# A recommendation tower: GpSimd's pair products and diagonals wait for VectorE's adds, with four diagonal buffers and z0 in one VectorE instruction

## The chip, the cores and the metric

The kernel runs on one core of a Trainium2 chip. The metric is the device time of one execution, in microseconds (us). The core has TensorE (PE, with its weight loads PEld), VectorE (DVE), ScalarE (ACT), GpSimd (POOL) and the queue engine SyncE (SP), each with a program of its own; they meet through semaphores.

## The reference

512 samples have 39 looked-up embeddings of 16 numbers each. Three layers of a compressed interaction network (CIN) follow, then two dense layers and an output.

```python
e = jnp.stack([tbl_f[ids[:, f]] for f in range(39)], axis=1)      # B=512, F=39, D=16

def cin_layer(X0, Xi, W, b):                                      # H = 128
    Wr = W.reshape(H, F0, Fi)
    return jnp.einsum('hjk,bjd,bkd->bhd', Wr, X0, Xi) + b[None, :, None]

Xi, res = e, []
for W, b in Ws:                       # three layers
    Xi = cin_layer(e, Xi, W, b)
    res.append(Xi.sum(axis=2))        # z0, z1, z2: 128 wide each
h = jnp.concatenate([*res, dense_ctx], axis=1)
h = relu(h @ W_top1 + b_top1); h = relu(h @ W_top2 + b_top2); y = h @ W_top3
```

Everything is float32.

## The kernel before

A column is one pair (sample, d); 512 × 16 columns make 16 groups of 512 columns (32 samples), and a group is four tiles of 128 columns (s = 0 to 3, eight samples each). All engines run the same loop over groups g, tiles s and ten chunks c of a tile; p = 10 s + c is the chunk's number in its group. The first group, the last and the two or three before it are written out, the others are one hardware loop. While group g is worked on, the first CIN layer of group g+1 is prepared, and the embeddings of group g+2 are gathered.

*TensorE.* `t_chunk` (L433) makes 512 columns of the second layer's weights times x1 (384 in chunk 9) in one of five PSUM banks, with three matmuls (high and low parts, L444 to L446). It waits until the chunk that used the bank five chunks before has been scaled. In between come: seven `pair_product`s for the next group (L412), after the chunks of `PAIR_AT`; four transposes of the next x0 after chunk 8 (L420); and after chunk `G_AT` of a tile the small product `g_product` (L429), x2 of two tiles before times a diagonal.

*ScalarE* scales chunks 0, 1, 3, 5, 7, 9 by x0t (L579), one instruction for each of the up to four 128-wide units of a chunk; it also copies x0t (L544), the small products (L566), and makes x1 of the next group with its bias and high part (L552, L561).

*VectorE* does chunks 2, 4, 6, 8 as multiply-adds onto ScalarE's results (L672, four instructions a chunk). Between them stand the five adds that sum the tile before over j (`sum_over_j`, L693): 1536 elements ("big"), 768, 384, 128 and a last 128 into x2, placed by `SUM_AT`; and the low part of x1 (L661, `lo`).

*GpSimd*, in this order within a group: `form_pairs` (L345) multiplies two factors of 117 × 512 for the next group's seven pair products, at the chunks of `FORM_AT` (6, 10, ..., 30); `diagonal` (L332) spreads x0t of a tile over a mask, at chunk 5 of each tile; `gather` (L322) issues ten indirect DMAs, at `GATHER_AT`; `index` makes their addresses at chunk 37; and `sum_z0` (L354, L357) sums x1 over d for z0 by halving, after tile 1. A position p in the code only orders GpSimd's own instructions. What they wait for are data and free buffers: a pair product for its factors and for the buffer of the pair two before it, a diagonal for the small product of two tiles before.

*SP* waits until all seven pairs of a group are formed and its gathers have landed, stores the gathered rows to scratch memory, loads them again as `rep`, copies `rep` twice and three times to `first`, and then six times to `second`; the first pair product of the next group waits for that chain.

After the last group the third layer's sum over all j follows in one block, then the dense layers.

Of the kernel before, what the change touches and what calls it, by code (L numbers as in the profile page):

```python
# [24 lines left out]
B, F, D, H = 512, 39, 16, 128  # L25
P = 128
# [30 lines left out]
RED = 5  # L57
# [13 lines left out]
FORM_AT = [6 + 4 * b for b in range(BLOCKS)]  # L71
PAIR_AT = [p + 5 for p in FORM_AT]
X0T_AT = 8
AHEAD = 2
GATHER_AT = [1, 3, 7, 9, 13, 15, 19, 21, 25, 27]
INDEX_AT = 37
G_AT = 5
G_COPY_AT = 7
# [3 lines left out]
HALVINGS = 3  # L82
Z0_TILE = 1
SUM_AT = (1, 3, 5, 6, 7)


def tower_program(nc, ids, starts, table, dense_t, pair_a, pair_b, w1, w2, b0, b1, b2,
# [6 lines left out]
    with ctx:  # L94
# [19 lines left out]
        diag = sb("diag", [P, 2, TB, J1])  # L114
# [50 lines left out]
        g_psum = small_bank[:, 0:TB * J1].rearrange("p (b j) -> p b j", b=TB)  # L165
# [24 lines left out]
        halved = sem("halved")  # L190
# [116 lines left out]
        def _(pool):  # L307
# [18 lines left out]

            def diagonal(t, slot, first):

                pool.wait_ge(x0t_ready, t + 1)
                if not first:  # L330
                    pool.wait_ge(g_mm, t - 1)
                pool.tensor_tensor(  # L332
                    diag[:, slot % 2, :, :],
                    x0t[:, slot:slot + 1, :].to_broadcast([P, TB, J1]),
                    mask[:, :].unsqueeze(2).to_broadcast([P, TB, J1]), ALU.mult).then_inc(diag_ready, 1)
# [11 lines left out]

            def sum_z0(g):

                pool.wait_ge(x1_lo_ready, (g + 1) * len(PIECES))  # L350
                by_d = x1[:, :].rearrange("p (b d) -> p b d", d=D)
                n, halvings = D // 2, 0
                while n > 1:
                    pool.tensor_tensor(by_d[:, :, 0:n], by_d[:, :, 0:n], by_d[:, :, n:2 * n], ALU.add).then_inc(halved, 1)  # L354
                    n, halvings = n // 2, halvings + 1
                    pool.wait_ge(halved, g * HALVINGS + halvings)
                pool.tensor_tensor(z0[:, bass.ds(g * GB, GB)].unsqueeze(2), by_d[:, :, 0:1], by_d[:, :, 1:2],  # L357
                                   ALU.add).then_inc(z0_ready, 1)
# [9 lines left out]
            def group(g, first=False, last=False, gathers=True, then_index=True):  # L368
                for s in range(TILES_PER_GROUP):
                    t = g * TILES_PER_GROUP + s  # L370
                    for c in range(CHUNKS):
                        p = s * CHUNKS + c
                        if c == G_AT:
                            diagonal(t, s, first and s < 2)
                        if p in FORM_AT and not last:
                            form_pairs(g + 1, FORM_AT.index(p))
                        if p in GATHER_AT and gathers:
                            gather(GATHER_AT.index(p))
# [414 lines left out]
```

## Time and profile before

| | us |
|---|---|
| median of 3 timed runs | 769.84 (767.8 to 770.15) |
| the profiled execution: its time | 767.13 |
| its span (first to last instruction) | 765.3 |
| TensorE busy | 674.8 (88%) |
| VectorE busy | 644.9 (84%) |
| ScalarE busy | 505.4 (66%) |
| GpSimd busy | 503.5 (66%) |

The span is the time between the first and the last instruction in the trace; some 2 us lie around it. Busy time doesn't count waits, but an instruction that has started and is held up counts as busy. The mean granted TensorE clock is 0.969 of full speed.

### The profile page before, as it was taken

What the parts mean: (1) busy time and instruction counts of PE and PEld (TensorE: products, weight loads), DVE (VectorE), ACT (ScalarE), POOL (GpSimd) and SP (SyncE); (2) the same over time, 40 slices, a digit from 0 to 9 for tenths busy, and PEclk for the clock granted to TensorE, in tenths of its full rate; (3) what the DMA queues carried; (4) which work ended last, traced back from release to release, by engine and by line L of the source; (5) the groups of instructions that cost most, each with busy time, mean ns of one, the idle gap of its engine ahead of it and who ended that gap; (6) DMA issues with size and microseconds to landing.
All of it is one profiled execution on the core that took longest, in us unless ns stands there. A gap on an engine that the chain in (4) does not pass through costs nothing. (4 is left out here: it accounts for less than half of the span.)

```text
span 765.3 us, 12277 instructions
## 1 busy us (share of the span) xinstructions
PE 674.8 (88%) x2525; PEld 470.0 (61%) x2525; DVE 644.9 (84%) x1425; ACT 505.4 (66%) x1700; POOL 503.5 (66%) x437
## 2 busy tenths in 40 slices
PE   2678999889898989989898979799898989999898
PEld 0246766657575757657675756576665667775463
DVE  0448899879898997999898989789899889999890
ACT  2055777658584966767585858577676758797572
POOL 6739596676859594967677685958688674422830
PEclk9899999999999998999999999999999999999999
DMA  6452121212121212212131312112130212000310
GB/s 194 95 147 54 32 80 15 82 23 74 28 69 40 69 40 43 67 20 84 16 86 20 77 29 69 40 39 70 20 90 10 78 28 78 23 1 1 92 39 0
DMA packets 54165, 41.34 MB, mean 54 GB/s; under 512 B 33735, under 2 KB 39092, under 8 KB 54023
## 3 DMA queue, kind: packets, MB, share of 16 engines
q1 hardware_dynamic: 49030, 39.72, 18.0%
q0 software_dynamic: 5120, 1.47, 3.4%
q8 instruction: 5, 0.08, 0.0%
q14 instruction: 10, 0.07, 0.0%
HBM read 10.46 MB, written 1.28 MB: 15 GB/s over the span
## 5 line engine op out<-in xcount | busy, mean ns | idle before, releaser
L579 ACT ACTIVATE prod<-t_bank,x0t 128x128 f32<-128x128 f32 x1472 | 415.7, 387 | 173.2 <-PE t_bank L446 168.6
L672 DVE SCALAR_TENSOR_TENSOR prod<-t_bank,x0t,prod 128x128 f32<-128x128 f32 x1024 | 286.0, 339 | 47.3 <-PE t_bank L446 46.8
L444 PE MATMUL t_bank<-w_hi,x_hi 128*128 128x512 f32 (+1 forms) x640 | 312.0, 487 | 15.4 <-DVE prod L672 12.2
L322 POOL DMA_INDIRECT emb<-in_table,idx x160 | 218.4, 1365 | 61.8 <-issue 54.9
L445 PE MATMUL t_bank<-w_lo,x_hi 128*128 128x512 f32 (+1 forms) x640 | 252.6, 395 | 0.0
L446 PE MATMUL t_bank<-w_hi,x_lo 128*128 128x512 f32 (+1 forms) x640 | 251.9, 394 | 0.0
L444 PEld LDWEIGHTS t_bank<-w_hi,x_hi 128*128 128x128 f32 x640 | 124.2, 194 | 79.7 <-DVE prod L672 22.4
L412 PE MATMUL x_bank<-pairs,w_pair 117*128 117x512 f32 x224 | 123.8, 636 | 46.4 <-POOL pairs L345 44.2
L693 DVE TENSOR_TENSOR partial<-partial 128x768 f32<-128x768 f32 (+2 forms) x192 | 155.7, 811 | 0.1
L445 PEld LDWEIGHTS t_bank<-w_lo,x_hi 128*128 128x128 f32 x640 | 124.3, 194 | 48.2 <-issue 27.6
L693 DVE TENSOR_TENSOR partial<-prod 128x1536 f32<-128x1536 f32 x64 | 132.7, 2073 | 15.2 <-ACT prod L579 9.0
L332 POOL TENSOR_TENSOR diag<-x0t,mask 128x320 f32<-128x320 f32 x64 | 58.4, 912 | 124.4 <-PE small_bank L429 124.4
L446 PEld LDWEIGHTS t_bank<-w_hi,x_lo 128*128 128x128 f32 x640 | 123.6, 193 | 25.0
L345 POOL TENSOR_TENSOR pairs<-first,second 117x512 f32<-117x512 f32 x90 | 121.6, 1351 | 4.8 <-PE x_bank L412 1.7
L412 PEld LDWEIGHTS x_bank<-pairs,w_pair 117*128 117x128 f32 x224 | 40.5, 194 | 70.5 <-POOL pairs L345 55.8
L566 ACT ACTIVATE G<-small_bank 128x320 f32 (+1 forms) x64 | 48.2, 753 | 6.4 <-PE small_bank L429 6.4
L693 DVE TENSOR_TENSOR x<-partial 128x128 f32<-128x128 f32 x64 | 47.7, 746 | 3.4
L354 POOL TENSOR_TENSOR x<-x 128x256 f32<-128x256 f32 (+2 forms) x48 | 48.0, 1000 | 3.0
L429 PE MATMUL small_bank<-diag,x 128*128 128x320 f32 x128 | 45.0, 432 | 1.6 <-DVE x L693 1.6
L727 DVE TENSOR_TENSOR w_hi<-G,w_hi 128x512 fp32r<-128x512 f32 x39 | 32.9, 912 | 2.3 <-ACT w_hi L627 2.3
L345 POOL TENSOR_TENSOR pairs<-first,rep 117x512 f32<-117x512 f32 x15 | 23.2, 1549 | 16.7 <-DMA first<-rep 16.7
L627 ACT ACTIVATE w_hi<-G 128x512 fp32r<-128x512 f32 x39 | 24.2, 631 | 8.7 <-PE t_bank L513 7.2
(66 smaller groups left out, 271.7 us busy)
## 6 DMA issues: line engine op xcount, KB each, us to landing
second<-rep SPq DMA_DIRECT2D x96, 234.0 KB
first<-rep SPq DMA_DIRECT2D x48, 78.0 KB
emb<-in_table,idx POOLq DMA_INDIRECT x160
G<-in_w SPq DMA_DIRECT2D x1, 2496.0 KB
w_ring<-in_w SPq DMA_DIRECT2D x13, 192.0 KB, 2.4
rep<-rep SPq DMA_DIRECT2D x28, 78.0 KB
rep<-emb_scratch SPq DMA_DIRECT2D x20, 78.0 KB
emb_scratch<-emb SPq DMA_DIRECT2D x16, 78.1 KB
```

Of the source, the lines that this page charges most:

```text
L322: pool.indirect_dma_start(out=emb[:, i * D:(i + 1) * D], out_offset=None, in_=table, in_offset=bass.IndirectOffsetOnAxis(ap=idx[:, i:i + 1 ...
L332: pool.tensor_tensor(diag[:, slot % 2, :, :], x0t[:, slot:slot + 1, :].to_broadcast([P, TB, J1]), mask[:, :].unsqueeze(2).to_broadcast([P, ...
L345: pool.tensor_tensor(pairs[:, b % 2, :], first[:, :], rep[0:PAIRS, :] if b == 0 else second[:, k, :], ALU.mult).then_inc(pair_ready, 1)
L354: pool.tensor_tensor(by_d[:, :, 0:n], by_d[:, :, 0:n], by_d[:, :, n:2 * n], ALU.add).then_inc(halved, 1)
L412: pe.matmul(x1_bank[:, :], w_pair[:, b * H:(b + 1) * H], pairs[:, b % 2, :], start=b == 0, stop=b == BLOCKS - 1).then_inc(pair_mm, 1)
L444: pe.matmul(acc, hi, w1_hi[:, cols], start=True, stop=False)
L445: pe.matmul(acc, hi, w1_lo[:, cols], start=False, stop=False)
L446: pe.matmul(acc, lo, w1_hi[:, cols], start=False, stop=True).then_inc(t_mm, 1)
L566: act.activation(G[:, :, bass.ds(g * GB + s * TB, TB)].rearrange("p j b -> p b j"), g_psum, ACT.Copy).then_inc(g_copied, 1)
L579: last = act.activation(prod[:, s % 2, SLOT[c] + u, :], t_bank[c % T_BANKS][:, u * H:(u + 1) * H], ACT.Copy, scale=x0t[:, s, j:j + 1])
L672: last = dve.scalar_tensor_tensor(unit, t_bank[c % T_BANKS][:, u * H:(u + 1) * H], x0t[:, s, j:j + 1], unit, ALU.mult, ALU.add)
L693: dve.tensor_tensor(out, left, right, ALU.add).then_inc(summed, 1)
```

## The change

- GpSimd's `form_pairs` and `diagonal` first call the new `beside_multiplies(t, c)`: they wait until VectorE has done the adds that stand before chunk c in its program. The positions `FORM_AT`, `PAIR_AT`, `DIAG_AT`, `GATHER_AT`, `SUM_AT` and `G_AT` move.
- `diag` has four buffers in place of two, and its axes are exchanged (j outer, sample inner), as are those of the small product in PSUM; ScalarE's copy of it no longer permutes. The diagonal waits for the small product of four tiles before.
- z0 moves from four adds on GpSimd (with semaphores between) to one `tensor_reduce` on VectorE, at chunk 4 of the group.

```diff
--- before.py
+++ after.py
@@ -68,20 +68,20 @@
 TOP1, TOP2 = 512, 256
 M1, M2 = TOP1 // P, TOP2 // P
 
-FORM_AT = [6 + 4 * b for b in range(BLOCKS)]
-PAIR_AT = [p + 5 for p in FORM_AT]
+FORM_AT = [6, 8, 12, 18, 22, 28, 32]
+PAIR_AT = [9, 11, 15, 21, 25, 31, 35]
+DIAG_AT = [2, 14, 24, 34]
 X0T_AT = 8
 AHEAD = 2
-GATHER_AT = [1, 3, 7, 9, 13, 15, 19, 21, 25, 27]
+GATHER_AT = [2, 2, 2, 8, 8, 14, 18, 20, 24, 28]
 INDEX_AT = 37
-G_AT = 5
-G_COPY_AT = 7
+G_AT = 2
+G_COPY_AT = 5
 BIAS_AT = 5
 X1_LO_AT = 36
 X1_LO_LAST_AT = 2
-HALVINGS = 3
-Z0_TILE = 1
-SUM_AT = (1, 3, 5, 6, 7)
+Z0_AT = 4
+SUM_AT = (2, 4, 6, 6, 8)
 
 
 def tower_program(nc, ids, starts, table, dense_t, pair_a, pair_b, w1, w2, b0, b1, b2,
@@ -111,7 +111,7 @@
         first = sb("first", [PAIRS, COLS])
         second = sb("second", [PAIRS, SECOND_SLOTS, COLS])
         x0t = sb("x0t", [P, TILES_PER_GROUP, J1])
-        diag = sb("diag", [P, 2, TB, J1])
+        diag = sb("diag", [P, TILES_PER_GROUP, J1, TB])
         pairs = sb("pairs", [PAIRS, 2, COLS])
         x1 = sb("x1", [P, COLS])
         x1_hi = sb("x1_hi", [P, COLS], f32r)
@@ -162,7 +162,7 @@
         small_bank = pb("small_bank", [P, COLS])
         h1_bank = [x1_bank, x0t_bank, t_bank[2], t_bank[3]]
         h2_bank = [t_bank[1], t_bank[4]]
-        g_psum = small_bank[:, 0:TB * J1].rearrange("p (b j) -> p b j", b=TB)
+        g_psum = small_bank[:, 0:TB * J1].rearrange("p (j b) -> p j b", b=TB)
         x0t_psum = x0t_bank[:, 0:TILES_PER_GROUP * F].rearrange("p (s f) -> p s f", f=F)
 
 
@@ -187,7 +187,6 @@
         x1_ready = sem("x1_ready")
         x1_hi_ready = sem("x1_hi_ready")
         x1_lo_ready = sem("x1_lo_ready")
-        halved = sem("halved")
         z0_ready = sem("z0_ready")
         t_mm = sem("t_mm")
         act_scaled = sem("act_scaled")
@@ -324,15 +323,22 @@
                     in_offset=bass.IndirectOffsetOnAxis(ap=idx[:, i:i + 1], axis=0),
                 ).then_inc(gathered, 16)
 
+            def beside_multiplies(t, c):
+
+                done = sum(at < c for at in SUM_AT)
+                if isinstance(t, int) and (t - 1) * RED + done <= 0:
+                    return
+                pool.wait_ge(summed, (t - 1) * RED + done)
+
             def diagonal(t, slot, first):
 
                 pool.wait_ge(x0t_ready, t + 1)
                 if not first:
-                    pool.wait_ge(g_mm, t - 1)
+                    pool.wait_ge(g_mm, t - TILES_PER_GROUP + 1)
                 pool.tensor_tensor(
-                    diag[:, slot % 2, :, :],
-                    x0t[:, slot:slot + 1, :].to_broadcast([P, TB, J1]),
-                    mask[:, :].unsqueeze(2).to_broadcast([P, TB, J1]), ALU.mult).then_inc(diag_ready, 1)
+                    diag[:, slot, :, :],
+                    x0t[:, slot, :].unsqueeze(2).to_broadcast([P, J1, TB]),
+                    mask[:, :].unsqueeze(1).to_broadcast([P, J1, TB]), ALU.mult).then_inc(diag_ready, 1)
 
             def form_pairs(g, b):
 
@@ -345,18 +351,6 @@
                 pool.tensor_tensor(pairs[:, b % 2, :], first[:, :], rep[0:PAIRS, :] if b == 0 else second[:, k, :],
                                   ALU.mult).then_inc(pair_ready, 1)
 
-            def sum_z0(g):
-
-                pool.wait_ge(x1_lo_ready, (g + 1) * len(PIECES))
-                by_d = x1[:, :].rearrange("p (b d) -> p b d", d=D)
-                n, halvings = D // 2, 0
-                while n > 1:
-                    pool.tensor_tensor(by_d[:, :, 0:n], by_d[:, :, 0:n], by_d[:, :, n:2 * n], ALU.add).then_inc(halved, 1)
-                    n, halvings = n // 2, halvings + 1
-                    pool.wait_ge(halved, g * HALVINGS + halvings)
-                pool.tensor_tensor(z0[:, bass.ds(g * GB, GB)].unsqueeze(2), by_d[:, :, 0:1], by_d[:, :, 1:2],
-                                   ALU.add).then_inc(z0_ready, 1)
-
             for g in range(AHEAD):
                 index(g, first=g == 0)
                 for i in range(GATHERS):
@@ -370,16 +364,18 @@
                     t = g * TILES_PER_GROUP + s
                     for c in range(CHUNKS):
                         p = s * CHUNKS + c
-                        if c == G_AT:
-                            diagonal(t, s, first and s < 2)
+                        if p in DIAG_AT:
+                            beside_multiplies(t, c)
+                            diagonal(t, s, first)
                         if p in FORM_AT and not last:
+                            beside_multiplies(t, c)
                             form_pairs(g + 1, FORM_AT.index(p))
-                        if p in GATHER_AT and gathers:
-                            gather(GATHER_AT.index(p))
+                        if gathers:
+                            for i, at in enumerate(GATHER_AT):
+                                if at == p:
+                                    gather(i)
                         if p == INDEX_AT and then_index:
                             index(g + AHEAD + 1)
-                    if s == Z0_TILE:
-                        sum_z0(g)
 
             group(0, first=True)
             with pool.Fori(1, GROUPS - AHEAD - 1) as g:
@@ -427,7 +423,7 @@
                 if not (isinstance(t, int) and t == 0):
                     pe.wait_ge(g_copied, t)
                 pe.matmul(small_bank[:, 0:TB * J1], x2[:, slot % 2, :],
-                          diag[:, slot % 2, :, :].rearrange("p b j -> p (b j)"),
+                          diag[:, slot, :, :].rearrange("p j b -> p (j b)"),
                           start=True, stop=True).then_inc(g_mm, 1)
 
             def t_chunk(t, s, c, first_tile, then_x0t):
@@ -453,7 +449,7 @@
                         p = s * CHUNKS + c
                         t_chunk(t, s, c, first and s == 0, g + 1 if p == X0T_AT and not last else None)
                         if c == G_AT and not (first and s < 2):
-                            g_product(t - 2, s)
+                            g_product(t - 2, (s - 2) % TILES_PER_GROUP)
                         if not last:
                             if p == X0T_AT:
                                 transpose_x0(g + 1, False)
@@ -480,7 +476,7 @@
             with pe.Fori(1, GROUPS - 1) as g:
                 group(g)
             group(GROUPS - 1, last=True)
-            g_product(TILES - 2, 0)
+            g_product(TILES - 2, 2)
 
 
 
@@ -495,7 +491,7 @@
                     pe.wait_ge(act_scaled, TILES * NA)
                     pe.wait_ge(dve_scaled, TILES * ND)
                 if m == M1 - 1:
-                    g_product(TILES - 1, 1)
+                    g_product(TILES - 1, 3)
                 first_layer(m, P, 0, z0[:, :], start=True)
                 first_layer(m, D, 3, dense[:, :])
 
@@ -563,8 +559,7 @@
             def copy_g(t, g, s):
 
                 act.wait_ge(g_mm, t + 1)
-                act.activation(G[:, :, bass.ds(g * GB + s * TB, TB)].rearrange("p j b -> p b j"),
-                               g_psum, ACT.Copy).then_inc(g_copied, 1)
+                act.activation(G[:, :, bass.ds(g * GB + s * TB, TB)], g_psum, ACT.Copy).then_inc(g_copied, 1)
 
             def scale_chunk(t, s, c, first):
 
@@ -673,6 +668,12 @@
                                                     x0t[:, s, j:j + 1], unit, ALU.mult, ALU.add)
                 last.then_inc(dve_scaled, 1)
 
+            def sum_z0(g):
+
+                dve.wait_ge(x1_ready, g + 1)
+                dve.tensor_reduce(z0[:, bass.ds(g * GB, GB)], x1[:, :].rearrange("p (b d) -> p b d", d=D),
+                                  AX.X, ALU.add).then_inc(z0_ready, 1)
+
             def sum_over_j(t, slot, i, first):
 
                 if i == 0:
@@ -703,8 +704,11 @@
                             split_x1_lo(g + 1, 0)
                         if p == X1_LO_LAST_AT:
                             split_x1_lo(g, 1)
-                        if c in SUM_AT and not (first and s == 0):
-                            sum_over_j(t - 1, s + 1, SUM_AT.index(c), first and s < 3)
+                        if p == Z0_AT:
+                            sum_z0(g)
+                        for i in range(RED):
+                            if SUM_AT[i] == c and not (first and s == 0):
+                                sum_over_j(t - 1, s + 1, i, first and s < 3)
 
             dve.wait_ge(w_loaded, 16 * 3)
             dve.tensor_tensor(w_pair[:, :], pair_a_raw, pair_b_raw, ALU.add).then_inc(w_pair_ready, 1)
```

## Rows read from the trace of the kernel before

**Rows 1.** Busy time by stretch: groups 1 to 13, then group 14.

```profile
93.30:638.34 545.04, 492.27 (x1899) 354.64 (x1899) 493.17 (x1120) 381.34 (x1340) 394.61 (x335) 0.97 0.21 50
638.34:674.62 36.28, 36.11 (x148) 26.72 (x147) 35.21 (x88) 29.24 (x105) 16.20 (x15) 1.00 0.14 46
```

**Rows 2.** Costliest groups of instructions, on the page: the GpSimd work of the change.

```profile
L332 POOL TENSOR_TENSOR diag<-x0t,mask 128x320 f32<-128x320 f32 x64 | 58.4, 912 | 124.4 <-PE small_bank L429 124.4
...
L345 POOL TENSOR_TENSOR pairs<-first,second 117x512 f32<-117x512 f32 x90 | 121.6, 1351 | 4.8 <-PE x_bank L412 1.7
...
L354 POOL TENSOR_TENSOR x<-x 128x256 f32<-128x256 f32 (+2 forms) x48 | 48.0, 1000 | 3.0
```

**Rows 3.** Waits over the span: us in total, times, longest.

```profile
DVE prod L672 <- PE t_bank L446: 46.8, 26, 5.3
PE x_bank L412 <- POOL pairs L345: 44.2, 21, 3.5
```

**Rows 4.** The line of VectorE's adds: ns at least, median, at most.

```profile
L693 DVE TENSOR_TENSOR partial<-prod x64: 1757/1759/3677, 54.6 to 704.7; 128x1536 f32<-128x1536 f32 x64
```

**Rows 5.** VectorE's timeline: start, duration, instruction, idle before it.

```profile
259.08 1.76 DVE L693 TENSOR_TENSOR partial<-prod 128x1536 f32<-128x1536 f32 x1
...
260.76 1.12 DVE L672 SCALAR_TENSOR_TENSOR prod<-t_bank,x0t,prod 128x128 f32<-128x128 f32 x4
...
262.00 0.95 DVE L693 TENSOR_TENSOR partial<-partial 128x768 f32<-128x768 f32 x1
...
263.90 0.55 DVE L693 TENSOR_TENSOR partial<-partial 128x384 f32<-128x384 f32 x1
...
267.31 1.80 DVE L693 TENSOR_TENSOR partial<-prod 128x1536 f32<-128x1536 f32 x1
...
275.23 2.22 DVE L693 TENSOR_TENSOR x<-partial 128x128 f32<-128x128 f32 x1
...
609.68 1.13 DVE L672 SCALAR_TENSOR_TENSOR prod<-t_bank,x0t,prod 128x128 f32<-128x128 f32 x4 [1.59 <-PE t_bank L446]
...
646.06 1.76 DVE L693 TENSOR_TENSOR partial<-prod 128x1536 f32<-128x1536 f32 x1
```

**Rows 6.** GpSimd's timeline.

```profile
249.53 1.27 POOL L345 TENSOR_TENSOR pairs<-first,second 117x512 f32<-117x512 f32 x1
...
263.87 1.72 POOL L345 TENSOR_TENSOR pairs<-first,rep 117x512 f32<-117x512 f32 x1 [0.34 <-DMA first<-rep]
...
267.32 1.21 POOL L322 DMA_INDIRECT emb<-in_table,idx  x1 [0.30 <-issue]
...
274.73 1.24 POOL L322 DMA_INDIRECT emb<-in_table,idx  x1 [0.19 <-issue]
...
276.00 1.29 POOL L345 TENSOR_TENSOR pairs<-first,second 117x512 f32<-117x512 f32 x1
...
646.08 2.89 POOL L345 TENSOR_TENSOR pairs<-first,second 117x512 f32<-117x512 f32 x1 [1.74 <-PE x_bank L412]
```

**Rows 7.** TensorE's timeline.

```profile
286.27 2.08 PE L412 MATMUL x_bank<-pairs,w_pair 117*128 117x512 f32 x2 [2.58 <-POOL pairs L345]
...
607.73 1.12 PE L412 MATMUL x_bank<-pairs,w_pair 117*128 117x512 f32 x2 [1.15 <-POOL pairs L345]
...
638.44 0.39 PE L446 MATMUL t_bank<-w_hi,x_lo 128*128 128x512 f32 x1
...
639.12 0.39 PE L446 MATMUL t_bank<-w_hi,x_lo 128*128 128x512 f32 x1
...
640.12 0.40 PE L445 MATMUL t_bank<-w_lo,x_hi 128*128 128x512 f32 x1
...
644.91 1.02 PE L412 MATMUL x_bank<-pairs,w_pair 117*128 117x512 f32 x2
```

**Rows 8.** Stretches with the granted clock (the share after the five engines).

```profile
287.00:291.00 4.00, 4.00 (x10) 2.81 (x9) 1.23 (x5) 0.38 (x2) 3.49 (x3) 0.50 0.04 2
608.00:612.00 4.00, 4.00 (x17) 2.81 (x16) 2.38 (x9) 1.72 (x6) 3.79 (x4) 1.00 0.22 62
```

## The prediction

> **What bounds the kernel now.** I read the stretch windows first. From VectorE's first multiply-adds of group 1 to those of group 14 lie 545.0 us, 13 groups that also gather, 41.93 us each. Group 14, which forms pairs but gathers nothing, takes 36.28, and TensorE is busy for 36.11 of it [rows 1]. So 36.3 is TensorE's own work for a group, and 5.6 us a group are lost elsewhere. The reader should see two losses. Pair products and the z0 sums on GpSimd are dear [rows 2], and the list of waits shows TensorE idle for GpSimd's pairs (44.2 us) and VectorE idle for TensorE (46.8) [rows 3]. And VectorE's adds stretch: the 1536-element add lasts 1.76 us at least, 3.68 at most [rows 4]. The timelines show what stretches them: the 128-element add of 275.23 took 2.22 and ended right behind the pair product of 276.00 to 277.29; the big add of 646.06, begun 0.02 before a pair product, kept its 1.76, and the pair product took 2.89 [rows 5, 6]. A gather alone leaves an add alone (1.80 against a gather of 1.21 [rows 5, 6]). So VectorE is delayed by GpSimd, TensorE by both, and all three are near their limit in turn.
>
> **The steps, part by part.** Times below are counted in one steady group from TensorE's chunk 0; I follow the instructions in order, because mean busy time can't tell which wait ends last.
>
> Prices. A chunk is 0.68 us of TensorE; the small product adds about 0.55; from a pair product that TensorE waited for to the next chunk's multiply-adds are 1.95 (607.73 to 609.68), to the next chunk's slot about 1.67 [rows 5, 7]. On VectorE, start to start: big add 1.68, four multiply-adds 1.04, 768 add 0.87; the 384 and 128 adds in a row about 0.9 with their wait [rows 5]. GpSimd: pair 1.27 to 1.29, diagonal 0.9 on average, gather 1.24 plus 0.2 to 0.3 between [rows 2, 6]; the last pair of a group to the first of the next 13.07 (250.80 to 263.87), the DMA chain through the scratch [rows 6]. A hand-over to GpSimd by semaphore I take as 0.1, an estimate: TensorE's pair product of 644.91 ended at 645.93 and GpSimd's of 646.08 began 0.15 later [rows 6, 7].
>
> *z0.* GpSimd loses the four adds: 48.0 us for three of the four kinds over 16 groups, 3.0 each [rows 2], plus gaps. VectorE gains one reduction over 512 elements. The trace has none. Bounds: the 384-element add, 0.55, and the 1536-element add, 1.76 [rows 5]; it is nearest the first, by the slope between them 0.68. It delays the first pair of the next group by as much, since it stands before the 768 add. With 1.76, each group would be 1.1 longer.
> "VectorE: DVE Perf Modes", section Rules for kernel authors, of the Trainium skill advises against this step: a reduction has only the plain mode and is called the slowest operation. Here the fp32 adds run at the same 1.05 ns an element [rows 5], so by the rule as by the row the sum stays 0.68.
>
> *The waits.* Pair products at chunks 8, 18, 28 now wait until VectorE has done the 384 and 128 adds behind the multiply-adds of chunk 6 of the same tile; those at 2 wait for the last add of the tile before, the one at 6 for the 768 add. TensorE wants each three chunks on, where it was five. Behind a waiting pair product on GpSimd stand the gathers; behind those the next pair product; and the SP queue waits for the last pair before it stores and reloads. The chain for tiles 1 and 2 is then a loop: multiply-adds 2 start, 1.04 + 1.68 + 1.04 + 0.87 + 1.04 + 0.9 = 6.6, semaphore 0.1, pair 1.27, TensorE 0.05, next tile's multiply-adds 1.95: 9.9 us a tile. TensorE alone needs 36.3 / 4 = 9.1.
>
> *Walk through a group.*
> Tile 0: multiply-adds at 2.2; big add to 5.1; multiply-adds, z0, 768 add to 7.8. GpSimd meanwhile: diagonal, three gathers (one is held by the big add), free at 7.7. Pair 0 from 7.9 to 9.15; TensorE wanted it at 7.7 (ten chunks, the small product, the transposes): **stall 1.5**. The 384 add is held to 9.15, both end at 9.9; pair 1 from 10.0 to 11.3; TensorE reaches it at 11.55.
> Tile 1: multiply-adds at 13.3, big add due at 14.35. But two gathers came between, so pair 2 starts at 14.25 and goes first: big add ends 17.1 instead of 16.1 (**1.0 on the path**). 384 and 128 done 20.8, pair 3 ends 22.2; TensorE had been ready at 20.9: **stall 1.4**.
> Tile 2: again two gathers before pair 4. It starts 25.2, the big add 25.2. Either order costs the same: big add ends 28.1 and pair 4 is on time, or pair 4 is 1.4 late and the add is not. Pair 5 ends 33.15, TensorE ready 31.5: **stall 1.7**.
> Tile 3: gather, pair 6 ends 35.9, beside multiply-adds. Pair product 6 on TensorE near 37.5, bias, hi, lo follow, and TensorE starts the next group after 41.3. First pair of the next group: 35.9 + 13.1 = 49.0, that is 7.7 into it, just in time.
> Check: 36.3 + 1.5 + 1.4 + 1.7 + 0.4 (restart and lo) = **41.3** against 41.93. The stretching of adds goes from the trace, save some 2 us a group, but the freed VectorE waits for TensorE, which waits for gated pairs.
> At tile 2, a gather with a pair product behind it shows a subtlety: the add at 275.23 was held to the end of a pair product that is recorded only from 276.00 [rows 5, 6]. "SBUF — State Buffer", section Who interferes with whom, of the Trainium skill says that whichever starts first keeps the shared port for the whole instruction; by recorded starts that would let the add pass. By the rule tile 2 comes 0.15 shorter, by the row as above; the sum can't tell.
>
> *Group 14* has no gathers, so no collisions at pairs 2 and 4: 41.3 − 2.05 = 39.25, but it stood at 36.28: **+3.0**. *Group 0*: the first pair waits for its data as before; it is asked for two chunks earlier, and the pair loop after it is a little shorter: taken as 0, within 2 either way. *Group 15* loses small waits and gains z0: 0. *Four diagonal buffers*: the diagonal's waits on the small product (124.4 us [rows 2]) vanish, but no row has anyone waiting for the diagonal; its new order of axes has no row; between 0.7 and, if doubled, 1.8, it stands beside a multiply-add of 1.12 [rows 5], so it costs 0 to 0.7; I take 0. ScalarE's copy without permutation stays off the path: ScalarE has 29.24 of 36.28 busy in group 14 [rows 1]. Moved small products and gathers: as many as before.
>
> Sum: 13 × (41.3 − 41.93) = −8.2; +3.0; 0; total −5.2. The profiled execution took 767.13; 761.9, and with the 2.7 by which the median of the timed runs lies above it, **765 us**. Bounds: a step error of 0.1 at each of eight serial steps is 0.8 a group or 10 us; z0 at 1.76 is +15.
>
> **Rivals.**
> *No collisions.* If the gathers finish before multiply-adds 2 of tiles 1 and 2, or pairs 2 and 4 slip in a free slot, the group is 39.25, 13 × (−2.7) + 3.0 = −32: **738 us**. For it: 0.15 us decides at tile 1. Against it: each of two gathers needs 1.5 and the gap is 1.7 + 1.04.
> *The waits are free*, TensorE bounds, as in group 14: 36.9 with restarts, 13 × (−5.0) + 0.6 = −65: **705 us**. For it: VectorE's uncontended work, 4 × 7.7 from the prices above and 1.9 for z0 and lo, 32.7 a group. Against: the loop of 9.9 a tile, in which nothing overlaps.
> *Slower: TensorE's clock.* After the stall of 2.58 before 286.27 the granted clock was 0.50 (1.2 GHz) in 287 to 291; after one of 1.15 before 607.73 it stayed at 1.00 (2.4 GHz) [rows 7, 8]. The new stalls, 1.4 to 1.7, lie between. If one a group lowers the clock, the pair product and chunk behind it take about twice as long, 1.5 more on the path, and a group is 42.8: 13 × 0.9 + 3.0 + 2 = +17: **787 us**. It decides from about 0.5 us a group upward.
> *Slower: the gate itself.* If each gated pair ends 0.35 later than I walk (longer semaphore, z0 dearer), four of them make 1.4, a group 42.7: +13: **783 us**.
> *It doesn't do what it says*: gates already open when GpSimd arrives. Excluded at chunks 8, 18, 28, where VectorE's chain ends last; open at 12, 22, 32.
>
> **How the numbers follow.** Walk as forecast, 755 to 775: 0.45, of which somewhat more than half faster. No collisions: 0.17. Free waits: 0.05. Clock: 0.17. Dearer gates: 0.16. A measurement here tells 0.3%, 2.3 us. Faster: 0.17 + 0.05 + 0.26 = 0.48; slower: 0.33 + 0.04, 0.36 rounded; same 0.16. The range 738 to 788 takes in all but the free waits and the tails, some 0.15.
>
> **What would show it.** Right: 1536-element adds at 1.76 in tiles 0 and 3, near 2.8 in tiles 1 or 2; three TensorE waits on the pairs a group of 1.4 to 1.7; the sum of TensorE's waits on pairs above 44.2; VectorE's busy time down by 50 us or more while its idle time for TensorE grows as much; group 14 slower than 36.28. Wrong: TensorE's pair waits near zero (free waits), adds all at 1.76 (no collisions), a granted clock below the present mean, or the reduction above 1 us.

## The result, and the profile after

| us | before | after |
|---|---|---|
| median of the timed runs | 768.82 (4 runs) | 783.48 (780.32 to 783.94, 4 runs) |
| span of the profiled execution | 765.3 | 782.1 |

The ratio of after to before is 1.0182, 95% interval 1.0147 to 1.0216: the change makes the kernel slower by 1.8%. I had forecast 765, with a chance of 0.36 for slower. All times here and below are of executions in the faster of the device's two states, which leaves out one run, 771.85 of the kernel without the waits.

First the same stretches as [rows 1], from VectorE's first multiply-adds of group 1 to those of group 14 and on to those of group 15.

```profile
93.67:648.20 554.53, 492.64 (x1901) 344.78 (x1899) 463.00 (x1132) 373.49 (x1340) 355.82 (x286) 0.99 0.20 49
648.20:689.40 41.20, 38.22 (x147) 27.37 (x146) 33.27 (x87) 28.50 (x104) 11.60 (x12) 0.96 0.13 41
```

Thirteen gathering groups take 554.5 in place of 545.0, 42.66 each for 41.93; group 14 takes 41.20 for 36.28. Together 14.4 of the 16.8 by which the span grew. Of the other 2.4, by these cuts 0.4 stand ahead of group 1 and 2.0 behind group 14. But the big add used to stand ahead of the multiply-adds at which I cut, and now stands behind them; that moves 1.7 from the front to the back, so it is group 0 and what comes before it that are some 2 longer. TensorE's busy time in the 13 groups is the same, 492.6 for 492.3; VectorE's fell by 30. So no engine has more to do. The waits say where the time is now:

```profile
DVE prod L667 <- PE t_bank L442: 115.0, 64, 9.1
...
PE x_bank L408 <- POOL pairs L351: 61.1, 46, 3.3
...
POOL pairs L351 <- DVE partial L694: 43.7, 44, 3.0
```

VectorE waits 115 us for TensorE, where it was 46.8, TensorE 61 for GpSimd's pairs, where it was 44.2 [rows 3], and GpSimd's pairs 44 for VectorE's adds, a row that the kernel before doesn't have. Three engines wait for one another in a ring. The costly groups of the change on the page, to set beside [rows 2]:

```profile
L338 POOL TENSOR_TENSOR diag<-x0t,mask 128x320 f32<-128x320 f32 x64 | 48.1, 751 | 181.3 <-DVE partial L694 117.8
...
L351 POOL TENSOR_TENSOR pairs<-first,second 117x512 f32<-117x512 f32 x90 | 115.5, 1284 | 45.9 <-DVE partial L694 43.7
```
The source line of the reduction (ns at least, median, at most):

```profile
L674 DVE TENSOR_REDUCE z<-x x16: 674/675/678, 49.3 to 693.5; 128x512 f32 x14, 128x32 f32<-128x512 f32 x2
```

The reduction takes 0.675, as sized. One group shows the ring. VectorE's timeline first, with start, duration, instruction and the idle time ahead of it:

```profile
264.29 1.12 DVE L667 SCALAR_TENSOR_TENSOR prod<-t_bank,x0t,prod 128x128 f32<-128x128 f32 x4 [0.58 <-PE t_bank L442]
...
270.91 1.31 DVE L694 TENSOR_TENSOR partial<-partial 128x384 f32<-128x384 f32 x2
...
275.76 1.13 DVE L667 SCALAR_TENSOR_TENSOR prod<-t_bank,x0t,prod 128x128 f32<-128x128 f32 x4 [1.88 <-PE t_bank L442]
...
276.80 2.83 DVE L694 TENSOR_TENSOR partial<-prod 128x1536 f32<-128x1536 f32 x1
...
282.50 0.87 DVE L694 TENSOR_TENSOR partial<-partial 128x384 f32<-128x384 f32 x2
...
286.81 1.13 DVE L667 SCALAR_TENSOR_TENSOR prod<-t_bank,x0t,prod 128x128 f32<-128x128 f32 x4 [1.87 <-PE t_bank L442]
...
297.88 1.12 DVE L667 SCALAR_TENSOR_TENSOR prod<-t_bank,x0t,prod 128x128 f32<-128x128 f32 x4 [1.87 <-PE t_bank L442]
...
306.69 1.12 DVE L667 SCALAR_TENSOR_TENSOR prod<-t_bank,x0t,prod 128x128 f32<-128x128 f32 x4 [0.58 <-PE t_bank L442]
```
GpSimd's timeline in tiles 0 and 1:

```profile
268.85 1.21 POOL L321 DMA_INDIRECT emb<-in_table,idx  x1 [0.30 <-issue]
...
270.21 1.26 POOL L351 TENSOR_TENSOR pairs<-first,rep 117x512 f32<-117x512 f32 x1 [0.15 <-issue]
...
272.44 1.30 POOL L351 TENSOR_TENSOR pairs<-first,second 117x512 f32<-117x512 f32 x1 [0.97 <-DVE partial L694]
...
275.47 1.21 POOL L321 DMA_INDIRECT emb<-in_table,idx  x1 [0.30 <-issue]
...
276.71 1.30 POOL L351 TENSOR_TENSOR pairs<-first,second 117x512 f32<-117x512 f32 x1
...
283.54 1.26 POOL L351 TENSOR_TENSOR pairs<-first,second 117x512 f32<-117x512 f32 x1 [0.88 <-DVE partial L694]
```
TensorE's, where it had waited:

```profile
261.84 0.49 PE L440 MATMUL t_bank<-w_hi,x_hi 128*128 128x512 f32 x1 [0.46 <-ACT prod L574]
...
271.52 1.13 PE L408 MATMUL x_bank<-pairs,w_pair 117*128 117x512 f32 x2 [1.61 <-POOL pairs L351]
...
284.85 1.13 PE L408 MATMUL x_bank<-pairs,w_pair 117*128 117x512 f32 x2 [1.26 <-POOL pairs L351]
...
295.92 1.13 PE L408 MATMUL x_bank<-pairs,w_pair 117*128 117x512 f32 x2 [1.25 <-POOL pairs L351]
```

The multiply-adds of chunk 2 open the four tiles at 264.29, 275.76, 286.81 and 297.88, the next group at 306.69: 42.40 a group. TensorE stands 1.61 before pair 0 (271.52), 1.26 before pair 3, 1.25 before pair 5; after each, VectorE's next multiply-adds come 1.96 to 4.24 later. The pair product of 276.71 stands behind a gather and goes ahead of the big add of 276.80, which takes 2.83. Both are as I walked them. In four of the thirteen groups the granted clock also falls behind the 1.61:

```profile
264.29:306.69 42.40, 37.49 (x149) 26.11 (x147) 35.97 (x88) 28.77 (x104) 26.79 (x23) 1.00 0.20 49
314.00:318.00 4.00, 4.00 (x9) 2.67 (x10) 2.23 (x7) 1.10 (x5) 2.67 (x3) 0.57 0.18 57
271.00:275.00 4.00, 3.48 (x12) 2.12 (x13) 2.85 (x7) 1.46 (x7) 2.85 (x3) 1.00 0.23 71
655.00:659.00 4.00, 3.79 (x8) 2.49 (x9) 2.37 (x7) 0.86 (x4) 2.72 (x3) 0.61 0.15 53
```

The first row is the group shown, at 1.00 throughout; the last is behind the stall of 1.44 in group 14. In 314 to 318 the clock is 0.57 on average, partly at 1.2 GHz; behind the same stall of 271.52 it stayed at 1.00 (2.4 GHz). Such a group takes 42.9: tile 0 is 1.6 longer, but the collision of tile 1 falls away. One more group, the ninth, takes 43.9: GpSimd stood 2.98 ahead of a gather, for which the trace names no cause, and TensorE 2.74 for the pair product behind it.

### The profile page after: what moved, and what is told of

Read it like the earlier page. It is cut to its first block, busy times and chain, and to the rows that moved or that the text cites. A ratio compares the mean times of both kernels' runs of the same rounds, so it can differ in the third digit from the quotient of the medians.

```text
span 782.1 us, 12310 instructions
## 1 busy us (share of the span) xinstructions
PE 676.1 (86%) x2525; PEld 460.3 (59%) x2525; DVE 609.5 (78%) x1441; ACT 496.0 (63%) x1700; POOL 450.7 (58%) x373
## 3 DMA queue, kind: packets, MB, share of 16 engines
q0 software_dynamic: 5120, 1.47, 2.9%
## 4 chain that ended last, share of the span: by engine, by line
DVE 31%; PE 22%; POOL 20%; issue 18%; DMA 4%; SPq 1%; DVEq 1%; ACT 1%; POOLq 0%; ACTq 0%
DVE prod L667 16%; DVE partial L694 11%; POOL emb L321 11%; PE x_bank L408 8%; POOL pairs L351 8%; PE t_bank L440 3%; PE t_bank L442 3%; PE t_bank L441 3%; DVE w_hi L731 3%; POOL diag L338 2%; DMA emb<-in_table,idx 2%; PE t_bank L520 1%; DMA second<-rep 1%; DVE x_lo L656 1%; PE t_bank L484 1%
## 5 line engine op out<-in xcount | busy, mean ns | idle before, releaser
L667 DVE SCALAR_TENSOR_TENSOR prod<-t_bank,x0t,prod 128x128 f32<-128x128 f32 x1024 | 287.1, 342 | 115.2 <-PE t_bank L442 115.0
L440 PE MATMUL t_bank<-w_hi,x_hi 128*128 128x512 f32 (+1 forms) x640 | 315.5, 493 | 13.6 <-ACT prod L574 6.0
L321 POOL DMA_INDIRECT emb<-in_table,idx x160 | 227.0, 1419 | 42.7 <-issue 37.4
L408 PE MATMUL x_bank<-pairs,w_pair 117*128 117x512 f32 x224 | 125.1, 641 | 63.5 <-POOL pairs L351 61.1
L338 POOL TENSOR_TENSOR diag<-x0t,mask 128x320 f32<-128x320 f32 x64 | 48.1, 751 | 181.3 <-DVE partial L694 117.8
L351 POOL TENSOR_TENSOR pairs<-first,second 117x512 f32<-117x512 f32 x90 | 115.5, 1284 | 45.9 <-DVE partial L694 43.7
L694 DVE TENSOR_TENSOR partial<-prod 128x1536 f32<-128x1536 f32 x64 | 136.1, 2126 | 0.1
L694 DVE TENSOR_TENSOR partial<-partial 128x768 f32<-128x768 f32 (+2 forms) x192 | 123.7, 644 | 2.3
L562 ACT ACTIVATE G<-small_bank 128x320 f32 (+1 forms) x64 | 29.1, 455 | 7.3 <-PE small_bank L425 7.3
L694 DVE TENSOR_TENSOR x<-partial 128x128 f32<-128x128 f32 x64 | 32.1, 502 | 0.0
L425 PEld LDWEIGHTS small_bank<-diag,x 128*128 128x128 f32 x128 | 23.4, 188 | 10.6 <-DVE x L694 5.3
L540 ACT ACTIVATE x0t<-x0t_bank 128x39 f32<-128x39 f32 x64 | 13.3, 214 | 25.0 <-DVE prod L667 15.5
```

The costliest lines, as they stand in the source:

```text
L321: pool.indirect_dma_start(out=emb[:, i * D:(i + 1) * D], out_offset=None, in_=table, in_offset=bass.IndirectOffsetOnAxis(ap=idx[:, i:i + 1 ...
L338: pool.tensor_tensor(diag[:, slot, :, :], x0t[:, slot, :].unsqueeze(2).to_broadcast([P, J1, TB]), mask[:, :].unsqueeze(1).to_broadcast([P, ...
L351: pool.tensor_tensor(pairs[:, b % 2, :], first[:, :], rep[0:PAIRS, :] if b == 0 else second[:, k, :], ALU.mult).then_inc(pair_ready, 1)
L408: pe.matmul(x1_bank[:, :], w_pair[:, b * H:(b + 1) * H], pairs[:, b % 2, :], start=b == 0, stop=b == BLOCKS - 1).then_inc(pair_mm, 1)
L425: pe.matmul(small_bank[:, 0:TB * J1], x2[:, slot % 2, :], diag[:, slot, :, :].rearrange("p j b -> p (j b)"), start=True, stop=True).then_i ...
L440: pe.matmul(acc, hi, w1_hi[:, cols], start=True, stop=False)
```

## The experiments

Ratios are to the kernel before, run on the same chip.

| kernel | median us | ratio, 95% interval | us a group, 1 to 13 | group 14 |
|---|---|---|---|---|
| after | 783.48 | 1.0182 (1.0147 to 1.0216) | 42.65 | 41.2 |
| no gates | 759.14 | 0.9866 (0.9828 to 0.9904) | 41.18 | 37.8 |
| z0 alone | 758.07 | 0.9860 (0.9832 to 0.9888) | 41.10 | 36.1 |
| diagonals alone | 767.15 | 0.9984 (0.9961 to 1.0007) | 41.73 | 36.0 |
| gates alone | 774.39 | 1.0080 (1.0048 to 1.0111) | 42.35 | 35.8 |
| gates off at 8 | 769.72 | 1.0012 (0.9988 to 1.0036) | 41.28 | 38.7 |
| pairs one later | 753.41 | 0.9788 (0.9747 to 0.9829) | 40.71 | 36.7 |
| pairs later | 731.65 | 0.9539 (0.9494 to 0.9585) | 39.23 | 36.8 |
| pairs later, no gates | 744.50 | 0.9693 (0.9666 to 0.9720) | 38.98 | 37.8 |
| gathers moved | 759.69 | 0.9884 (0.9848 to 0.9919) | 40.99 | 39.6 |
| both moved | 748.66 | 0.9782 (0.9715 to 0.9849) | 40.54 | 36.8 |
| later, last gather moved | 745.47 | 0.9717 (0.9687 to 0.9747) | 40.21 | 36.8 |
| z0 later | 793.33 | 1.0301 (1.0227 to 1.0375) | 43.28 | 39.0 |

The last two columns are from the profiles: between the big adds of tile 0 of groups 1, 14 and 15. The granted clock adds a spread of its own: in the profiles of "pairs one later", "pairs later, no gates", "gates off at 8" and "z0 later" it was at half for 20.5 us in the closing block, which then lasts 69.1 to 69.4 us from the last big add instead of about 61. The columns by group are free of this.

### No gates

```diff
                         if p in DIAG_AT:
-                            beside_multiplies(t, c)
                             diagonal(t, s, first)
                         if p in FORM_AT and not last:
-                            beside_multiplies(t, c)
                             form_pairs(g + 1, FORM_AT.index(p))
```

> The changed kernel with the two calls of beside_multiplies taken out, nothing else: order, buffers, z0 on VectorE as changed. Theory (the waits for VectorE's adds, followed three chunks later by TensorE's demand, set the group): TensorE's waits on GpSimd's pairs fall below 30 us, the adds stretch again (a 1536-element add of over 3 us somewhere), and the time is 750 to 772. Rival (the new positions and the gathers between them cost the time, gates or no gates): 778 to 788. Second rival (the stretched adds cost more than the gates did): over 788.

24 us less than the changed kernel, by the median of three runs from 757.0 to 765.3; the profiled one is the slowest of them, its span 18.7 shorter. So the waits themselves are the loss, and all the rest of the change together is a gain of 1.3%. The waits of TensorE for pairs all but go (61.1 before this edit), and those of VectorE for TensorE fall (115.0):

```profile
DVE prod L665 <- PE t_bank L440: 69.0, 68, 9.2
...
PE x_bank L406 <- POOL pairs L351: 2.0, 1, 2.0
```

As the theory had it, adds stretch again. By the source line of the big adds, then by the costly groups of the page:

```profile
L692 DVE TENSOR_TENSOR partial<-prod x64: 1739/1747/3401, 66.1 to 702.6; 128x1536 f32<-128x1536 f32 x64
```
The page:

```profile
L692 DVE TENSOR_TENSOR partial<-partial 128x768 f32<-128x768 f32 (+2 forms) x192 | 150.3, 783 | 2.3
L692 DVE TENSOR_TENSOR partial<-prod 128x1536 f32<-128x1536 f32 x64 | 117.9, 1843 | 0.1
```

The longest big add is 3.4 us, but that is a rare one: on average they take 1.84, less than the 2.13 of the changed kernel, which forces a collision in tiles 1 and 2. It is the small adds that stretch. All adds together (with 39.6 for the last ones) take 307.8 us; the changed kernel has 136.1 + 123.7 + 32.1 = 291.9, the kernel before 336.1. So the waits save 16 us of stretched adds and cost 24 us of time: here held adds cost less than ordered ones.

### z0 alone

The new `sum_z0` on VectorE at chunk 4 and the old one gone, in the kernel before.

> The kernel before with z0 as one reduction on VectorE at chunk 4, and nothing else of the change. Theory: GpSimd is rid of about 3.9 us a group, TensorE's wait of 2.6 for the fifth pair product and the low clock after it go; 13 groups of about 39.5 to 40.5, 740 to 755. Rival (VectorE sets the group before too, so 0.68 more on it is paid): 772 to 780.

The gain is 10.6 us, less than I expected: TensorE's waits for pairs go, and VectorE, busy for 679.6 of 756.4 us (90%, where it was 84%), takes their place. Part of that is that GpSimd's pair products, with z0 gone, meet other adds: all adds together take 365.2 us where they took 336.1. Its profile has 41.1 a group, and these waits:

```profile
PE t_bank L429 <- DVE prod L657: 37.2, 42, 1.5
...
PEld x_bank L397 <- POOL pairs L344: 4.9, 3, 2.9
```

Its adds of 768, 384 and 128, which took 155.7 us before:

```profile
L684 DVE TENSOR_TENSOR partial<-partial 128x768 f32<-128x768 f32 (+2 forms) x192 | 210.8, 1098 | 0.1
```

### Diagonals alone

Four buffers, the exchanged axes, the plain copy, in the kernel before.

> The kernel before with four diagonal buffers, the axes of the diagonal and of the small product exchanged, and ScalarE's copy without permutation; nothing else. Theory: the diagonal's waits on the small product (124 us) go, nobody waited for it, no change: 765 to 772. Rival (GpSimd comes to its pair products earlier, and they meet other adds): 2 to 8 away on either side.

No change that can be told, as priced; the copy fell from 0.75 to 0.46 (below), off the path.

### Gates alone, and gates off at 8

```diff
 # gates alone: the kernel before
                         if c == G_AT:
+                            beside_multiplies(t, c)
                             diagonal(t, s, first and s < 2)
                         if p in FORM_AT and not last:
+                            beside_multiplies(t, c)
                             form_pairs(g + 1, FORM_AT.index(p))
 # gates off at 8: the changed kernel
-                            beside_multiplies(t, c)
+                            if c != 8:
+                                beside_multiplies(t, c)
                             form_pairs(g + 1, FORM_AT.index(p))
```

> The kernel before with the waits for VectorE's adds in front of every pair product and diagonal, in its own positions, with TensorE's pairs five chunks on, z0 on GpSimd and two diagonal buffers. Theory (the waits are cheap where five chunks lie between): the 1536-element adds return to 1.76 for the most part, and the time is 750 to 768. Rival (GpSimd is late already with z0 and the gathers, so every wait is passed on to TensorE): 774 to 795.

> The changed kernel without the waits for VectorE's adds ahead of the pair products of chunks 8, 18 and 28; the waits of the other four pair products and of the diagonals stay. Theory (these three are the ones that stand at the end of VectorE's chain; the others are open when GpSimd comes): TensorE's two waits of 1.25 a group go and the adds stretch again, near the 762 of the kernel without any such wait: 755 to 770. Rival (the waits of the diagonals and at 6 hold up the gathers and cost as much): 774 to 784.

With five chunks between the product and its use the waits cost 0.8%, my rival's side, not my theory's. Nor did the big adds return to 1.76: they take 2.05 on average, for 2.07 before. TensorE waits once a group, 58.2 us in 15 times, for the pair product behind z0. From the waits, then from GpSimd's and TensorE's timelines:

```profile
PE x_bank L421 <- POOL pairs L352: 58.2, 15, 5.0
```
GpSimd:

```profile
285.68 1.88 POOL L361 TENSOR_TENSOR x<-x 128x256 f32<-128x256 f32 x2
...
290.35 1.27 POOL L352 TENSOR_TENSOR pairs<-first,second 117x512 f32<-117x512 f32 x1
```
TensorE:

```profile
291.67 1.43 PE L421 MATMUL x_bank<-pairs,w_pair 117*128 117x512 f32 x2 [4.04 <-POOL pairs L352]
```

GpSimd, held up before, comes to z0 and that pair later. Without the three waits at chunk 8 the changed kernel has 41.28 a group for 42.65, as the theory had it: by the profiles the waits cost 1.47 a group in all and these three 1.37. The time falls by less, 14 us of the 24, since this profile has 8 us of low clock in its closing block; its ten runs all lie between 766 and 772.

### Pairs later, by one chunk and by two

```diff
-PAIR_AT = [9, 11, 15, 21, 25, 31, 35]
+PAIR_AT = [10, 12, 16, 22, 26, 32, 35]     # one later
+PAIR_AT = [11, 13, 17, 23, 27, 33, 35]     # two later
```

> The changed kernel with the pair products of TensorE one chunk later instead of two (10, 12, 16, 22, 26, 32, 35). Theory (the distance is paid chunk by chunk while TensorE stands at a pair): the waits shorten, but the pair at 22 and 32 now stands behind chunk 2, so VectorE's next multiply-adds start without it; most of the gain of two chunks: 733 to 750. Rival (a slack of 0.68 covers only part of each 1.25): 752 to 768.

> The changed kernel with TensorE's pair products two chunks later (11, 13, 17, 23, 27, 33, the last still 35), gates kept. Theory (a loop of VectorE's chain, the gated pair product and TensorE's restart): the next tile's chunk 2 no longer stands behind the pair, TensorE's waits on pairs fall from 61 to under 20 us, a group to 39 to 40.5: 742 to 762. Rival (the three-chunk distance is no cause; TensorE waits there because VectorE is behind anyway): within 5 of 783.

Two chunks take 52 us off with every wait for the adds kept; one chunk takes 30, in the range of the rival: a slack of 0.68 covers a part of each wait, and the rest is paid. TensorE's waits for pairs fall from 61.1 to 31.1 with one chunk and to 10.1 with two, and with two it is busy for 485.9 of 510.0 us in groups 1 to 13, by the windows and the waits of the kernel with two:

```profile
87.85:597.80 509.95, 485.94 (x1901) 341.29 (x1899) 481.15 (x1132) 369.55 (x1340) 382.55 (x286) 1.00 0.22 54
```
The waits of the same kernel:

```profile
DVE prod L667 <- PE t_bank L442: 38.7, 81, 5.4
...
PE x_bank L408 <- POOL pairs L351: 10.1, 19, 2.0
```

This kernel beats both, the kernel before by 4.6%. It shows that the waits were not dear in themselves; what was dear was TensorE standing at the pair product ahead of the chunk that VectorE needs next.

### Pairs later, no gates

> The kernel with the pair products two chunks later, and without the two waits for VectorE's adds. It tells what the waits are worth when TensorE doesn't stand behind them. Theory (they keep pair products off the adds, and VectorE is near the bound): slower than 731.65 by 1 to 4%, 740 to 760. Rival (the waits only delay): 715 to 730.

By time the forecast came true: 744.50 lies in the theory's range, 13 us above the kernel that keeps the waits, and the two intervals of the ratio are far apart. The profile doesn't say why. Its groups are nearly the same, 38.98 for 39.23. Of the 10.3 by which its span is longer, 8.3 are the closing block at the low clock, 4.2 come before group 1, 1.0 in group 14, and the groups give back 3.2. It is also of the fastest of the five runs (739.42); the other four took 744 to 745 at a higher mean clock (0.984 to 0.989 for 0.977), so the low clock in the closing block can't be their reason, and no trace shows what is. That the waits pay once there is room is shown by the time; that they do it by keeping pair products off the adds is not shown.

### Gathers moved

```diff
-GATHER_AT = [2, 2, 2, 8, 8, 14, 18, 20, 24, 28]
+GATHER_AT = [2, 2, 2, 12, 12, 14, 22, 22, 24, 28]     # gathers moved; both moved, with pairs two later
+GATHER_AT = [2, 2, 2, 8, 8, 14, 18, 20, 24, 24]       # later, last gather moved
```

> The changed kernel with the gathers that stood ahead of the pair products of chunks 12 and 22 put behind them (12, 12, 14, 22, 22 for 8, 8, 14, 18, 20). Theory: pair products 2 and 4 no longer take the port before the 1536-element adds of tiles 1 and 2; those fall from 2.83 to 1.76, each 1.05 on the path, 13 times two: 27 less, 752 to 760. Rival (the stretched add is covered by the wait for the pair that follows): 778 to 785.

> The changed kernel with both edits: pair products two chunks later and the gathers behind the pair products of 12 and 22. Theory (with the loop open VectorE and TensorE are near their own work, so a stretched add of 1.1 in one tile a group is partly covered): 718 to 730, against 731.65 with the first edit alone. Rival (the two gains add up, 24 more): 705 to 712.

> The changed kernel with the pair products two chunks later, and the last gather at chunk 24 instead of 28. With the pairs later the one stretched 1536-element add (2.88) is that of tile 3, beside pair product 6, which a gather precedes. Theory: that add falls to 1.76 and tile 3 from 10.3 to about 9.3: 13 less, 716 to 724. Rival (the gather at 24 only moves the collision to another add, as when the gathers were moved behind pairs 2 and 4): 729 to 745.

The first gives 23.8 us for the 27 of the sum: the stretched adds of tiles 1 and 2 lay on the path. Big adds take 1.76 on average, for 2.13. Their tiles fall from 11.05 and 11.07 to 10.05 and 10.06, where the loop without collisions had been put at 9.9. But with the pairs later the same move makes it worse, 40.54 a group for 39.23, and so does the last gather at 24. My theories for both were wrong. For "both moved" the rival was too, as neither had a loss; its last adds of a tile, 128 elements, take 1.00 on average for 0.55 in "pairs later". For the last gather, the rival that the collision only moves had 729 to 745, and it took 745.47. VectorE's and GpSimd's timelines of that kernel show it:

```profile
280.40 2.23 DVE L694 TENSOR_TENSOR x<-partial 128x128 f32<-128x128 f32 x1
...
283.59 2.10 DVE L694 TENSOR_TENSOR partial<-prod 128x1536 f32<-128x1536 f32 x1
```
GpSimd:

```profile
279.96 1.21 POOL L321 DMA_INDIRECT emb<-in_table,idx  x1 [0.31 <-issue]
...
281.19 1.28 POOL L351 TENSOR_TENSOR pairs<-first,second 117x512 f32<-117x512 f32 x1
...
282.79 1.28 POOL L351 TENSOR_TENSOR pairs<-first,second 117x512 f32<-117x512 f32 x1 [0.32 <-DVE x L694]
```

The last add at 280.40, due for 0.28, is held to the end of the pair product of 281.19, and the big add after it by the next pair product.

### z0 later

```diff
-Z0_AT = 4
+Z0_AT = 8
```

> The changed kernel with the reduction for z0 at chunk 8 of the group instead of 4, behind the adds for which the first pair products wait. Theory (my walk: in tile 0 the reduction, 0.68, lies on the path to pair product 0 and 1): 14 times 0.6 to 0.68 less, 8 to 10: 773 to 776. Rival (TensorE's wait for the first pair is set by GpSimd's three gathers, which end at the same moment): 781 to 785.

Slower, which neither had forecast. Two of its four runs took 798 and 799, among them the profiled one, whose closing block ran at the low clock; the other two 787.6 and 788.5, still 4 to 5 above the changed kernel. The group is 0.6 longer: 0.3 in every one, the rest because seven groups take 0.5 more than the others, where four did, and one takes 47.1, for which I have no cause. GpSimd's third gather in tile 0 used to start just before the 768 add (268.85, the add at 269.01) and run 1.21; now the 768 add has already begun. VectorE:

```profile
270.27 0.95 DVE L694 TENSOR_TENSOR partial<-partial 128x768 f32<-128x768 f32 x1
...
272.17 1.86 DVE L694 TENSOR_TENSOR partial<-partial 128x384 f32<-128x384 f32 x1
```
GpSimd:

```profile
270.70 1.60 POOL L321 DMA_INDIRECT emb<-in_table,idx  x1 [0.30 <-issue]
...
272.33 1.27 POOL L351 TENSOR_TENSOR pairs<-first,rep 117x512 f32<-117x512 f32 x1
```

The gather takes 1.60, the pair product that must follow ends 7.46 after chunk 2's multiply-adds and not 7.18, and the add of 272.17 is held by it. So in tile 0 GpSimd's three gathers end last, by little, not VectorE's chain with z0 in it, as my walk had left open (7.7 and 7.8).

## Why the prediction was wrong

**Steps that held.** The prices of z0 (0.68; it was 0.675), of the adds and multiply-adds, the order of events in every tile, the two collisions (2.83 and 2.85 for the forecast 2.8), the three stalls (1.61, 1.25, 1.25 for 1.5, 1.4, 1.7, together 0.5 less than forecast), the free diagonal. The rise of TensorE's waits on pairs above 44.2 and of VectorE's on TensorE are as named. VectorE's busy time fell by 35, not by 50.

**The term that failed** is "41.3" in the walk through a group, in the sum "13 × (41.3 − 41.93) = −8.2". It measured 42.66, and the term is +9.5. By tiles, from one opening multiply-add to the next: 11.1, 10.85, 10.95 and 8.4 forecast; 11.47, 11.05, 11.07 and 8.81 measured, in all 1.1 more in a group at full clock. No step is missing; several are short:
- A hand-over from VectorE's add to GpSimd took 0.22 in tile 0 and 0.17 in tile 1 (the 384 and 128 adds of 270.91 ended 1.31 later, at 272.22, and the pair product began at 272.44; those of 282.50 at 283.37, and 283.54), not 0.1; the one row from which I had estimated it gave 0.15. The hand-overs of tiles 1 and 2 lie on the path, 0.15 a group; the one of 272.44 does not, as TensorE had its next chunk to do.
- The largest part is around TensorE's start of a group: from pair 0 to the next multiply-adds 4.24 for 4.1; from pair 5 to the next group's start 8.32 for 8.1 (295.92, then 304.24), from there to multiply-adds 2 2.45 for 2.2 (261.84, 264.29). The restart after a wait, for which I had one row, was right: 1.96 for 1.95.
- The three gathers of tile 0 freed GpSimd 8.2 after the group's start (268.85 + 1.21 = 270.06, less 261.84), not 7.7; a quarter of a microsecond of it is the late opening of the tile.
- The clock, and the one group of 43.9, 0.27 a group on average. As a rival I had put the clock at 1.5 in every group; it took 0.5 in four of them.

The check at the end of the walk should have told me. It added TensorE's side: 36.3 of its own work, 4.6 of stalls, 0.4 for the rest. Measured, in the group from 264.29 to 306.69 at full clock, it is 37.49 busy, 4.11 of stalls and 0.80 for the rest. The 36.3 is mis-sized by 1.2: I took it from group 14, which gathers nothing, while the 13 groups before the change had 492.27 / 13 = 37.9 [rows 1], and "pairs later", almost without stalls, has 37.4. Why a gathering group keeps TensorE busy for longer at the same clock is open. The stalls, forecast too long, hid a part of it.

I had written that "a step error of 0.1 at each of eight serial steps is 0.8 a group or 10 us". The error was 1.36 a group, 18 us, all in one direction, beyond the bound. It was taken as symmetric; that made the gain. Group 14 took 41.2 for the forecast 39.25, but for another reason. Its tiles are 12.9, 9.9, 9.9 and 8.6 for 11.1, 9.85, 9.9 and 8.4: without gathers the loop of 9.9 is right, and what is missing is tile 0, where the clock fell (0.61) behind the stall of 1.44. Group 0, taken as 0 within 2, cost about 2. So the sum is +9.5, +4.9 and +2.4, 16.8 for −5.2.

**The rivals.** "The gate itself", four gated pairs 0.35 later each, a group of 42.7 and 783 us, is what came in size. In mechanism it did so only in small part: the gates' hand-overs are 0.15 a group of the 1.36; that the number fits is partly luck. "No collisions" is a kernel that exists: gathers moved, 759.7 where I had 738: most of its groups take 40.4 where I had 39.25, short by the same 1.1, and in four of the 13 tile 0 is slower. "The waits are free", 36.9 a group, is no kernel here; "pairs later" has 39.23.

**What the change is made of,** by the runs: z0 alone −10.6, the diagonals nothing that can be told, the gates +24 in the new positions (783.5 against 759.1) and some +6 (0.8%) in the old. That held adds are the smaller evil when TensorE follows at three chunks (16 us of adds saved, 24 us of time lost) is shown by the kernel without gates; that the distance is the cause, by the two kernels with the pairs later. With the pairs two chunks later it is the other way round by time: 731.7 with the waits, 744.5 without.

## What to carry to other kernels

A wait put in to keep two engines off a shared resource makes one chain of them. Before adding it, count the ring: the producer's chain, the gated work, the consumer, and what of the consumer's program stands between it and the producer's next input. If that ring is longer than the busiest engine's own share, move the consumer's use of the gated work later (two chunks later, by one list, took 52 us off here) before anything else. In a hand walk of such a ring, give every hand-over the largest gap that the trace shows, and let the errors point one way.

## What was not expected of the hardware

- ScalarE's copy of the small product, 128 × 320 from PSUM to SBUF, took 0.75 us with its axes exchanged and 0.46 without. GpSimd's diagonal of the same size fell from 0.91 on average [rows 2] to 0.75, but its least was 0.72 before and is 0.735 now: it mostly no longer meets adds, and the exchanged axes gave it nothing. The source lines of ScalarE's copy, before (L566) and after (L562):

```profile
L566 ACT ACTIVATE G<-small_bank x64: 727/754/782, 76.4 to 711.8; 128x320 f32 x56, 128x320 f32<-128x320 f32 x8
L562 ACT ACTIVATE G<-small_bank x64: 437/455/458, 77.5 to 728.9; 128x320 f32 x56, 128x320 f32<-128x320 f32 x8
```
The diagonal, before (L332) and after (L338):

```profile
L332 POOL TENSOR_TENSOR diag<-x0t,mask x64: 718/944/1453, 50.5 to 699.9; 128x320 f32<-128x320 f32 x64
L338 POOL TENSOR_TENSOR diag<-x0t,mask x64: 735/740/1479, 48.3 to 716.3; 128x320 f32<-128x320 f32 x64
```

- A pair product right behind a gather on GpSimd holds VectorE's add from before its own recorded start: the last add of 280.40 above was held though the pair product is recorded from 281.19, 0.79 later. The section SBUF: two separate sides of "SBUF — State Buffer" in the Trainium skill has whichever starts first as the holder; these rows fit that only if the start is earlier than recorded. The fourteen traces agree: of the adds that only one pair product meets, recorded after the add's start, those with the pair product right behind a gather were held in 206 of 236 cases, at up to 0.89 after the start and never at 0.91 or more; with no gather right before it, none of 44 was held, at 0.02 to 1.73.
- After the same stall of 1.61 the clock fell in four groups and not in eight; and the closing block ran 20.5 us at half the clock in four profiles of fourteen, 8 us longer. What decides is open.
